# The same operations of a windowed-attention block in another order on all five engines

## The reference, cut to what matters

```python
xn = layernorm(xw)                                # over the 96 channels
q, k, v = qkv(xn)                                 # 12 heads of 8
attn = softmax(q * SCALE @ k.T + bias)            # 49 x 49 per head and window
x1 = x + proj(attn @ v)                           # back in image order
seq2 = bn(conv3x3_depthwise(x1))                  # one 3x3 filter per channel
out = seq2 + gelu(seq2 @ w1.T + b1) @ w2.T + b2   # hidden size 384
```

## Time and profile before

| | us |
|---|---|
| median of 3 runs | 3153.03 |
| lowest, highest | 3148.52, 3162.89 |
| the profiled run, its time | 3152.75 |
| its span in the profile | 3151.0 |
| PE busy, share of the span | 96% |
| DVE, ACT, POOL busy | 92%, 88%, 62% |

### The profile page before, as it was taken

How to read it: one execution, slowest core, us unless ns; L and a number is a source line. 1 busy time by engine, 2 the same in 40 slices (tenths; PEclk the granted TensorE clock), 3 DMA queues, 4 the chain that set the end, 5 groups by cost and what they waited for, 6 DMA issues and landing times.

```text
span 3151.0 us, 199775 instructions
## 1 busy us (share of the span) xinstructions
PE 3029.5 (96%) x88076; PEld 2108.1 (67%) x88076; DVE 2893.3 (92%) x4901; ACT 2777.0 (88%) x4869; POOL 1958.7 (62%) x2578
## 2 busy tenths in 40 slices
PE   5999999999999999999999999999999999999997
PEld 3666666666766666666666666766666666666664
DVE  5899999999999999999999999999999999999996
ACT  4799999998988999989898998998988999898986
POOL 3566666666666666666666666666666666666665
PEclk9999999999999999999999999999999999999998
DMA  2233333333333333333333333333333333333331
GB/s 65 82 97 92 96 95 91 97 93 94 94 92 96 91 98 90 96 90 95 96 91 96 91 96 94 93 96 91 96 91 93 93 95 94 93 97 92 95 92 43
DMA packets 269922, 288.31 MB, mean 92 GB/s; under 512 B 55651, under 2 KB 252580, under 8 KB 269062
## 3 DMA queue, kind: packets, MB, share of 16 engines
q1 hardware_dynamic: 235364, 198.14, 22.8%
q0 software_dynamic: 32768, 77.14, 7.0%
q10 hardware_dynamic: 930, 0.26, 0.0%
HBM read 39.34 MB, written 38.54 MB: 25 GB/s over the span
## 4 chain that ended last, share of the span: by engine, by line
PE 93%; issue 3%; ACT 1%; DVE 1%; SPq 1%; DMA 1%; POOL 1%; POOLq 0%; ACTq 0%; DVEq 0%
PE d_ps L271 22%; PE st_ps L315 12%; PE o_ps L361 11%; PE sm_ps L336 10%; PE b_ps L379 7%; PE b_ps L415 7%; PE a_ps L271 4%; PE b_ps L271 4%; PE a_ps L282 3%; PE a_ps L283 3%; PE a_ps L284 3%; PE d_ps L282 1%; PE b_ps L283 1%; PE d_ps L284 1%; PE d_ps L283 1%
## 5 line engine op out<-in xcount | busy, mean ns | idle before, releaser
L790 DVE SCALAR_TENSOR_TENSOR s<-ximg,cols,s 96x392 f32<-96x392 f32 x1792 | 1142.3, 637 | 30.7 <-POOL s L656 3.2
L764 DVE TENSOR_REDUCE mx<-sm_ps 128x12 f16<-128x588 f32 x1024 | 784.9, 767 | 131.6 <-PE sm_ps L336 128.8
L496 ACT ACTIVATE p<-st_ps 128x588 f32<-128x588 f32 x1024 | 672.4, 657 | 186.6 <-PE st_ps L315 183.5
L666 POOL DMA_DIRECT2D ox<-o_sb x1024 | 582.8, 572 | 28.5 <-ACT o_sb L521 14.9
L336 PEld LDWEIGHTS sm_ps<-k_all,q_all 127*49 127x49 f16 x24576 | 459.7, 103 | 172.3 <-issue 76.9
L271 PE MATMUL d_ps<-g,w_s 128*64 128x392 f32 x3072 | 558.3, 499 | 0.2 <-issue 0.2
L639 POOL TENSOR_TENSOR s<-ximg,cols 96x392 f32<-96x392 f32 x256 | 216.0, 844 | 524.4 <-DVE y L827 523.6
L315 PEld LDWEIGHTS st_ps<-q_all,k_all 128*49 128x49 f16 x24576 | 436.3, 103 | 157.8 <-issue 107.3
L315 PE MATMUL st_ps<-q_all,k_all 128*49 128x49 f16 x24576 | 517.3, 186 | 21.7 <-issue 19.5
L336 PE MATMUL sm_ps<-k_all,q_all 127*49 127x49 f16 x24576 | 508.1, 185 | 27.7 <-issue 17.9
L628 POOL TENSOR_TENSOR xl<-xn,xh 96x392 f16<-96x392 f32 x256 | 258.9, 1011 | 262.1 <-ACT xh L577 244.7
(11 more groups left out here) (126 smaller groups left out, 5959.3 us busy)
## 6 DMA issues: line engine op xcount, KB each, us to landing
ox<-o_sb POOLq DMA_DIRECT2D x1024, 73.5 KB
k_all<-kh SPq DMA_DIRECT2D x512, 75.0 KB
q_all<-qh SPq DMA_DIRECT2D x512, 75.0 KB
x_sb<-in_x SPq DMA_DIRECT2D x256, 147.0 KB, 2.4
out<-y SPq DMA_DIRECT2D x256, 147.0 KB
q_all<-ql SPq DMA_DIRECT2D x256, 75.0 KB
k_all<-kl SPq DMA_DIRECT2D x256, 75.0 KB
q_all<-mxt SPq DMA_DIRECT2D x256, 9.4 KB, 2.1
```

The lines of the kernel that those rows point to most:

```text
L496: af(p32[:, p, :, :].rearrange("p (b h) n -> p b h n", b=2), st_ps[:, :, 0:HALF].rearrange("p b (h n) -> p b h n", n=TOK), ACT.Exp).then_i ...
L666: nc.gpsimd.dma_start(ox[:, c % 2, x4, :], o_sb[x4::4, c % 2, :, :]).then_inc(o_in[c % 2], 16)
L764: v.tensor_reduce(mx[:, c % 2, 0:HEADS, p].rearrange("p (b h) -> p b h", b=2), sm_ps[:, :, 0:HALF].rearrange("p b (h n) -> p b h n", n=TOK ...
L790: v.scalar_tensor_tensor(acc, image_rows(c, k // 3, k % 3), cw_c[:, k:k + 1], acc, ALU.mult, ALU.add)\
```

## The change

Only the order of the calls in the five loops changes, and with it which operation is the first or the last of a group. PE now starts a step with the transpose and the hidden layer, has the three parts of the second product apart and in the order 1, 2, 0, the values before the variance, `values_times_p` in the order 1, 0, and the projection last. On SP the store moves into the middle of the six transfers, whose order becomes key high (row 2), key low, query high, store, query low, key high (row 0), query high (row 1); `first_term`'s wait now stands at the key's row 2. POOL has `second_product` before `first_product`, the addition directly behind them, then the two image parts, `to_channels`, and `input_low` behind these. On DVE and ACT most calls move. Offsets such as s - 5 for s - 6 go with the moves.

```diff
--- before.py
+++ after.py
@@ -248,15 +248,15 @@
                 sp.dma_start(dram_rows(out, c), y[0:C, c % 2, :]).then_inc(stored[c % 2], 16)
 
             for s in range(STEPS):
+                term(q_all, 1, qh, qh_done, s - 4)
+                maximum_row(s - 5)
                 load(s)
-                first_term(k_all, 0, kh, kh_done, s - 3)
-                term(k_all, 2, kh, kh_done, s - 3)
+                first_term(k_all, 2, kh, kh_done, s - 3)
+                term(k_all, 1, kl, kl_done, s - 3)
                 term(q_all, 0, qh, qh_done, s - 3)
+                store(s - 11)
                 term(q_all, 2, ql, ql_done, s - 3)
-                term(k_all, 1, kl, kl_done, s - 3)
-                term(q_all, 1, qh, qh_done, s - 3)
-                store(s - 11)
-                maximum_row(s - 4)
+                term(k_all, 0, kh, kh_done, s - 3)
             for r in stored:
                 sp.wait_ge(r, 16 * (CHUNKS // 2 + 1))
 
@@ -348,10 +348,10 @@
             def values_times_p(c, p):
                 if not real(c):
                     return
-                if p == 0:
+                if p == 1:
                     wait(pe, v32_done, c)
                 wait(pe, p_done[p], c)
-                if p == 0:
+                if p == 1:
                     free(pe, (o_done[1], c-1), (o_done[0], c-1))
                 elif p == 2:
                     free(pe, (o_done[0], c), (o_done[1], c-1))
@@ -436,36 +436,36 @@
                 if not real(c):
                     return
                 wait(pe, g_done[k], c)
-                if k == 0:
+                if k == 1:
                     free(pe, (g_done[0], c), (xn_done, c+7), (y_done, c-1))
-                halves(d_ps[0:128, 0:CT], w2_s[:, k, :], g[:, k, :], start=k == 0, stop=k == 2).then_inc(s_done[k], 1)
+                halves(d_ps[0:128, 0:CT], w2_s[:, k, :], g[:, k, :], start=k == 1, stop=k == 0).then_inc(s_done[k], 1)
 
             for s in range(STEPS):
-                exp_scores(s - 4, 2)
-                max_scores(s - 3, 3)
-                projection(s - 6)
+                maxima_rows(s - 3)
                 hidden(s - 8, 0)
-                maxima_rows(s - 3)
                 hidden(s - 8, 1)
                 hidden(s - 8, 2)
+                max_scores(s - 2, 0)
                 exp_scores(s - 4, 3)
-                max_scores(s - 2, 0)
-                second(s - 8, 0)
                 second(s - 8, 1)
+                max_scores(s - 2, 1)
                 second(s - 8, 2)
                 keys(s - 1)
-                max_scores(s - 2, 1)
+                max_scores(s - 2, 2)
                 queries(s - 1)
+                second(s - 8, 0)
                 exp_scores(s - 3, 0)
-                centred(s)
-                max_scores(s - 2, 2)
-                exp_scores(s - 3, 1)
                 values_times_p(s - 4, 2)
                 values_times_p(s - 4, 3)
+                centred(s)
+                exp_scores(s - 3, 1)
+                values(s - 2)
                 variance(s)
-                values(s - 2)
+                max_scores(s - 2, 3)
+                exp_scores(s - 3, 2)
+                values_times_p(s - 3, 1)
                 values_times_p(s - 3, 0)
-                values_times_p(s - 3, 1)
+                projection(s - 5)
 
 
 
@@ -515,7 +515,7 @@
 
                 if not real(c):
                     return
-                wait(act, pv_done[1 if half == 0 else 3], c)
+                wait(act, pv_done[0 if half == 0 else 3], c)
                 if half == 0:
                     wait_ring(act, o_in, c - 2, 64)
                 af(o_sb[:, c % 2, :, 2 * half * TOK:(2 * half + 2) * TOK],
@@ -577,26 +577,26 @@
                 af(xh[0:C, c % 2, :, 0:TOK], xn[:, :, :], ACT.Identity).then_inc(xh_done, 1)
 
             for s in range(STEPS):
+                input_high(s - 1)
                 gelu(s - 8, 2)
                 if real(s - 8):
                     act.preload_act_table_set("natural_log_exp_and_others")
                 exp(s - 4, 3)
                 key_high(s - 1)
+                outputs(s - 4, 0)
+                log_sums(s - 5)
+                inverses(s - 5)
                 query_high(s - 1)
                 exp(s - 3, 0)
-                log_sums(s - 5)
                 square(s)
-                inverses(s - 5)
+                outputs(s - 4, 1)
                 exp(s - 3, 1)
-                outputs(s - 4, 1)
                 log_variance(s)
                 root(s)
                 exp(s - 3, 2)
                 if real(s - 7):
                     act.preload_act_table_set("gelu_and_others")
                 gelu(s - 7, 0)
-                outputs(s - 3, 0)
-                input_high(s)
                 gelu(s - 7, 1)
 
 
@@ -681,13 +681,13 @@
                 tt(sl[:, :], s2[0:C, c % 2, :], sh[:, :], ALU.subtract).then_inc(sl_done, 1)
 
             for s in range(STEPS):
-                first_product(s - 6)
-                second_product(s - 6)
-                image_high(s - 7)
-                image_low(s - 7)
-                add_products(s - 6)
-                to_channels(s - 4)
                 input_low(s)
+                second_product(s - 5)
+                first_product(s - 5)
+                add_products(s - 5)
+                image_high(s - 6)
+                image_low(s - 6)
+                to_channels(s - 3)
 
 
 
@@ -822,7 +822,7 @@
 
                 if not real(c):
                     return
-                wait(dve, s_done[2], c)
+                wait(dve, s_done[0], c)
                 dve.wait_ge(stored[c % 2], (c // 2 + 1) * 16)
                 v.scalar_tensor_tensor(y[0:C, c % 2, :], d_ps[0:C, 0:CT], b2_c, s2[0:C, c % 2, :], ALU.add, ALU.add)\
                  .then_inc(y_done, 1)
@@ -849,25 +849,25 @@
                                        ALU.add, ALU.add).then_inc(sum_done, 1)
 
             for s in range(STEPS):
+                maxima(s - 2, 1)
+                tap(s - 7, 5)
+                tap(s - 7, 6)
+                key_low(s - 1)
+                tap(s - 7, 7)
+                block_out(s - 8)
+                tap(s - 7, 8)
+                query_low(s - 1)
+                normalise(s - 5)
                 maxima(s - 2, 2)
                 values_out(s - 2)
+                maxima(s - 2, 3)
                 input_normal(s)
-                maxima(s - 2, 3)
+                tap(s - 6, 2)
                 image_sum(s - 5)
-                tap(s - 6, 2)
                 maxima_out(s - 2)
                 tap(s - 6, 3)
                 tap(s - 6, 4)
                 maxima(s - 1, 0)
-                tap(s - 6, 5)
-                tap(s - 6, 6)
-                block_out(s - 7)
-                maxima(s - 1, 1)
-                key_low(s)
-                query_low(s)
-                tap(s - 6, 7)
-                tap(s - 6, 8)
-                normalise(s - 4)
```

## The result

The changed kernel takes 3167.73 us in the median of 16 runs, the kernel before 3156.30 (16 runs): ratio 1.0033, 95% interval 1.0021 to 1.0044. The profiled run took 3169.09 us with a span of 3167.3 us. The forecast was 3117 us, 1.2% faster. Measured is 0.3% slower, and the interval leaves out 1: the time lies inside the range of 3075 to 3185, but the change went the other way than forecast.

What follows compares the result with a forecast made beforehand. PE was taken as the bound, 11.56 us of own work per period plus 0.385 lost to late instructions. Terms -0.35 +0.09 +0.07 +0.05 = -0.14 per period, -36 us over 255 periods: 3117 us, range 3075 to 3185.

Steps and rivals of the forecast that it cites:

- supply of instructions: PE's 256-instruction packets come late in the dense stretch of score groups; spreading these groups gains 0.35 us per step.
- changes of pattern: On PE, switching between whole array, halves and quarters costs 0.09 us each; seven instead of six, +0.09 per step.
- two more f32 starts: On PE, the second product's three parts lie apart, adding two f32 group starts: +0.07 us per step.
- tight places: PE's handovers with other engines that have little or no room: +0.05 us per step together, bounds 0 and 0.3.
- SP's queue: Six transfers issued more than 3 us before max 0 wants them: no cost, up to 0.05 us if late.
- place 1: PE's max 1 needs sm_ps free: maxima of part 0 done at 2.95, wanted at 2.98; no room.
- place 2: PE's centred, at 7.1, needs DVE's output sum (L827), expected done at 7.0: room 0.1 us.
- rival B: A tight place on PE runs late by 0.1 to 0.25 us per step beyond 0.05: 3143 to 3181, chance 0.20.
- the 3.3 us: Supply time per 256-instruction packet on PE, set so the count returns the earlier loss: 0.37 us per step against 0.385 measured.
- Rival A: PE's own step doesn't grow, pattern changes and f32 starts being hidden: 3076 us, chance 0.10.
- C: PE's instruction supply wasn't late, or is as late in any order; the 0.35 gain vanishes: 3206 us, chance 0.09.
- D: DVE's tap 8 loses to POOL's first_product and takes 1.37, delaying PE's values by 0.65: 3283 us, chance 0.07.

Runs made afterwards that it cites:

- e4: Kernel before with exp_scores 3 moved between the second and third hidden part, adding two pattern changes per step: 3216.76 us, one run.
- e11: Changed kernel with the six transfers one behind the other and the store last, and filter tap 7 left out: 3132.45 us, ratio 0.9917 to the kernel before.
- e1: Changed kernel with SP's order alone changed, six transfers one behind the other and the store last: 3159.91 us, ratio 0.9950 to the kernel before.
- e2: Kernel before with the changed kernel's order of SP's calls alone: 3195.29 us, ratio 1.0065 to the kernel before.
- e3: Separate program of only 480 back-to-back exp_scores groups, transfers in the second half: 128 matmuls take 3.63 us without transfers, 3.80 with them.
- e10: e1 repeated unchanged on another chip: 3154.07 us, ratio 0.9972 to the kernel before.

## Why the prediction was wrong

Per step, as the prediction's sum had it, and as measured:

| term | predicted | measured | from |
|---|---|---|---|
| supply of instructions | -0.35 | -0.30 | 0.39 lost above the shortest period, then 0.205 less 0.114 |
| changes of pattern | +0.09 | +0.11 | what is left of 0.25; e4 |
| two more f32 starts | +0.07 | +0.03 | 0.69 + 0.69 + 0.66 against 2.00 |
| tight places | +0.05 | +0.11 | max 1 0.02, centred 0.08 to 0.09 (e11) |
| SP's queue | 0 | +0.11 | 0.114 before max 0; e1 and e2 give 0.05 to 0.11 |
| sum | -0.14 | +0.06 | +0.067 by the ruler |

The step that failed is the sentence on the SP queue, "No cost, and up to 0.05 per step if the last lands late now and then". It took over 3 us from issue to use as plenty. The landing has a median of 2.4 us, but a tail beyond 4, and with the store ahead of three transfers (the prediction counted two) the room fell from 4.4 to 3.8 us. The wait table of the kernel before had L336 waiting for q_all, 4.3 us in 6 times: the room was already at its edge. What does more, the store ahead, the shorter distance or the order of the six, the runs don't separate: e1 undoes them all. As it stands in front of max 0 this is 0.11 of the 0.2 us between forecast and result; taking it away gave back 0.05 to 0.10.

Second, the tight places. The walk found them (place 1 "No room", place 2 "Room 0.1") and put the output sum's end at 7.0, where 7.07 was measured. But it compared the sum's end with when PE wants centred, without what lies between the end of a DVE operation and the next start on PE: 0.06 for max 1, 0.11 to the load and 0.15 to the matmul for centred (the DVE and PE rows above). With that, no room is left. So rival B was right in its mechanism, but with 0.06 us beyond the 0.05 charged it is smaller than the 0.1 at which B begins. That its 3143 to 3181 holds the measured time is luck: the transfer's 0.11 brings it there. For max 1 the 0.02 is read off two distances, and no run tests it.

Third, what held. A stream of scores is held up by the supply of its instructions (e3), the kernel before lost 0.29 of its 0.38 us where such groups stand densest, and spreading them removes most of the gaps, 19.5 us in L315 to 0.4; -0.30 instead of -0.35. That the 3.3 us were fitted and not measured shows in e3's 3.6 to 3.8. The condition that the prediction named for its failure, more than 3.5 us per packet, was met in e3. The prediction's count gives 0.20 us per step for 3.8, and 0.09 was lost besides the transfer. Part of this smallness may be owed to the transfer itself, since in e1 and e10, without its wait, 0.133 to 0.155 are lost; whether instructions catch up while PE waits is argued and not shown. The f32 starts were charged too high. One such group costs 0.03 more behind scores (0.69 where it is 0.66 behind the queries), and of the three parts of the second product two stand behind scores now, where one did.

Rival A (the step doesn't grow) is out: the shortest period grew by 0.25. C (supply not the cause, or late in any order) is out by the issue gaps and by e3; here the trace speaks against the Trainium skill, Runtime: NRT & Kernel Launch, Instruction fetch mechanics, which has the crossing of a block mostly hidden: where 256 instructions take 1.89 us, at least 1.56 us more are seen in front of every block (e3). D (tap 8 loses to first_product) is out: tap 8 takes 0.61 us in every step, and the product pays:

```profile
L790 DVE SCALAR_TENSOR_TENSOR s<-ximg,cols,s 96x392 f32<-96x392 f32 x1792 | 1116.0, 623 | 23.2 <-POOL s L656 4.5
...
L656 POOL TENSOR_TENSOR s<-s,part 96x392 f32<-96x392 f32 x256 | 311.8, 1218 | 20.1
...
L639 POOL TENSOR_TENSOR s<-ximg,cols 96x392 f32<-96x392 f32 x256 | 278.2, 1087 | 791.9 <-DVE y L827 791.9
```

Its 1087 ns (844 before) and the addition's 1218 (1020 before) are hidden, since POOL has time; the tap fell from 637 to 623 ns. Keeping the two engines apart did spare DVE some work. The forecast held that this brings nothing, since PE doesn't wait for DVE. No run tests it, and e11 shows that the reason given is wrong: centred waits for the output sum in every step, so a tap that is shorter in front of it can count.

Of the 0.09 us per step that are left besides the transfer, 0.03 lie in front of the keys and 0.04 in L361 and the projection; part shows as issue, the rest I haven't traced to a cause.

The version that beats both kernels is e1, the new order with the six transfers together: 0.9950 and 0.9972 on two chips, both intervals below 1.

## What to carry over

Work out the room of a handover from the end of one operation to the start of the next with what lies between them, 0.06 to 0.15 us here, and for a transfer from the slow end of its landing, not from its median: a queue order that costs nothing on the median put 0.11 us per step in front of its reader in the mean. In the PE timeline a wait shorter than the overlap of matmul rows isn't marked; compare the distance of starts with the same group elsewhere, behind and in front of the same neighbours. And of an engine that is 91% busy, ask where its chain has no idle in front of a hand-back, not how much it is busy.

## What was not expected of the hardware

- A stream of small matmuls is limited by its instructions: 256 of them every 3.6 us in the mean (3.45 to 4.00), though they need 1.89, with 98 GB/s of other traffic adding 4% (e3).
- A transfer of 75 KB, the last of the six, lands 2.4 to 2.5 us after its issue in the median; one in ten takes more than 3.8 us and one in a hundred more than 4.7 us in the changed kernel. Issuing it takes 0.67 us, but over 1.5 in 8 of 256 cases, 2.04 in the sample at 2002.32.
- A change of the array's pattern costs about 0.1 us in PE's pipeline (e4: 0.22 for two), and in rows it is no gap.
- An f32 group costs 0.03 us more behind a group of scores than behind the queries (0.69 and 0.66).
- POOL's product beside a running tap of DVE: here the one that began later paid. The product began 0.22 us after tap 8 and took 1.09 us where its mean was 0.84 before; the tap kept its 0.61.
